# Rounding the first attention's weights on GpSimd: one instruction with two additions, or two with a multiplication and an addition each

## The chip, the cores and the metric

The kernel runs on one core of one Trainium2 chip. The metric is the device time of one execution in microseconds; the time before is the median of three runs. The profile is of one further execution, seen by the hardware profiler.

## The reference

Sixteen batch elements x[b] of 256 tokens by 256 features, each with a context of 77 tokens, pass through four blocks. Every element takes the same way, and until the recurrence no element needs another one.

```
block 0:  x = attention_q(ln1(x), itself)    + x      16 heads, quantised   ("a1")
          x = attention_q(ln2(x), context)   + x      16 heads, quantised   ("a2")
          x = geglu(ln3(x))                  + x
block 1:  x = x + attention(rms(x), itself)           ("sa")
          x = x + attention(rms(x), context)          ("ca")
          x = x + swiglu(rms(x))
block 2:  x = x + attention(ln(x), ln(tokens))        8 heads ("mh")
          u = (ln(x) @ W_in) @ B;  s_t = silu(A s_(t-1)) + u_t;  x = x + s @ C + ...
block 3:  one more attention over the context, softmax over the queries, and a layer norm
attention_q:  q, k, v rounded to 8 bits;  w = softmax(q k / 4)
              out = (round(w / d) clipped to 0..255) * d  @  v
```

The change is in `round(w / d)` of a1, the first attention. There the weights of one element are 16 heads x 256 queries x 256 keys.

## The kernel before

**Layout of the program.** It has three parts, one after the other: all sixteen elements through blocks 0 to 2 up to the recurrence's input; the recurrence; block 3. In the first part three elements are under way at a time ("streams"); each stream has buffers of its own (`work0`, `work1`, `work2`, which the profile shows as `work`).

**Who decides the order.** Each engine runs its instructions in the order in which they were written, and waits on semaphores. The order of the first part is made at build time by a small list scheduler (class `Plan`): `plan()` adds some 5,000 tasks, each with an engine, a cost in us written into the code, and the tasks it needs. `order()` starts always the task that can start earliest, and among equals the one of the oldest element and with the longest rest ahead. So a changed cost can move any task on any engine. A second plan, `plan3()`, does the same for block 3. In `plan()` a DMA transpose ("turn") occupies the queue of SyncE for `TURN` = 2.5 us, and the time in which a load or a store lands is a task of `LAND` = 2.5 us on an engine "clock" that doesn't exist on the chip.

**The first attention's chain.** a1 is done in 8 parts of an element (`(u, i)`: four units u of a half of the heads and a tile of 128 queries, two halves i each; a part is 128 queries x 4 heads x 256 keys = 128x1024). Each part goes: TensorE scores (L882) -> VectorE maximum (L1191, L1194) -> ScalarE exponentials (L1440, four instructions) -> VectorE reciprocal, factor (L1276, L1278) and four scalings to multiples of the step, clipped at 255 (L1285) -> GpSimd rounding (L775) -> SyncE's queue issues a DMA transpose (L687) -> TensorE weighs the values (L954), once for each half of the heads, when the four parts of that half have landed. The rounding adds 1.5 * 2^23 and takes it away again, which leaves the nearest whole number, and writes it as bf16:

```python
eng.tensor_scalar(rounded_part(a, u, i, p), e_part(a, u, i, p), MAGIC, -MAGIC, ALU.add, ALU.add)
```

There are two buffers for the scaled weights and two for the rounded ones (`HELD` = 2): the scores of a part stand in the plan behind the rounding two parts before it, and its rounding waits for the transpose two parts before it. Behind the weighing come ScalarE's L1462 (`xhat`), the output projection (L836), VectorE's residual (L1308), and the norm of the second attention. The second attention, a2, has 4 parts of 128x616; VectorE rounds these (L1296), and their transposes and weighing have the same lines 687 and 954, the weighing with 77 rows in place of 128.

**GpSimd's other work** in this part: the factor of each norm (L734), a bias added to the residual (L741), the spread of the rounded keys and queries (L749, L760), one scaling of a2's weights (L767), a memset (L728). In block 3, L1667 spreads the queries.

## Time and profile before

| | us |
|---|---|
| median of 3 runs (lowest, highest) | 3125.79 (3118.36, 3126.36) |
| the profiled execution's own time | 3128.91 |
| span of its trace, first to last instruction | 3127.2 |
| TensorE busy | 2520.2 |
| VectorE busy | 1899.8 |
| ScalarE busy | 1297.8 |
| GpSimd busy | 1023.1 |

PE is TensorE's matmuls and PEld its weight loads, DVE VectorE, ACT ScalarE, POOL GpSimd, SPq SyncE's queue. "Busy" is the time in which an instruction of the engine runs. The idle time before an instruction is put down to what ended it (the releaser); "issue" is time in which the engine waited for nothing that the profile shows. L775 is line 775 of the kernel.

### The profile page before, as it was taken

The numbers are of one execution on the slowest core, as the hardware profiler recorded it, in microseconds if no ns is written. First come the engines' busy times: TensorE is split into PE (matmuls) and PEld (weight loads), VectorE is DVE, ScalarE is ACT, GpSimd is POOL, SyncE is SP. The second block draws the span as 40 slices with busy tenths as digits, with TensorE's granted clock in tenths as the row PEclk, the third lists the DMA queues.
The fourth block names the chain that finished last, engine by engine and source line by source line (L and its number), as shares of the span: only waits on it lengthen the run. The fifth ranks groups of instructions, "written<-read, shape, count | busy, mean of one in ns | idle before, by whom it ended". The sixth has DMA issues, their size and how long they took to land. (4 is left out here: it accounts for less than half of the span.)

```text
span 3127.2 us, 47208 instructions
## 1 busy us (share of the span) xinstructions
PE 2520.2 (81%) x16568; PEld 1811.3 (58%) x16568; DVE 1899.8 (61%) x4639; ACT 1297.8 (42%) x3243; POOL 1023.1 (33%) x903
## 2 busy tenths in 40 slices
PE   4369888898888888898989898888888765448997
PEld 3247676666666766575767666666666442334443
DVE  4975666776766576868686767676764320004766
ACT  1534344545443345454444544344432211224654
POOL 3841132423242233343333334242321010005775
PEclk9679898898888989898989898979888765558999
DMA  4220011101111011111111111110110000001110
GB/s 187 45 52 10 20 18 24 38 21 21 31 31 24 18 28 31 31 25 27 35 24 29 30 24 28 23 28 22 28 25 7 5 18 23 0 0 34 35 37 22
DMA packets 222407, 90.45 MB, mean 29 GB/s; under 512 B 205280, under 2 KB 212784, under 8 KB 221424
## 3 DMA queue, kind: packets, MB, share of 16 engines
q1 hardware_dynamic: 215728, 67.68, 10.9%
q10 hardware_dynamic: 6464, 19.93, 1.7%
q8 instruction: 132, 2.16, 0.3%
q14 instruction: 83, 0.68, 0.1%
HBM read 27.80 MB, written 9.44 MB: 12 GB/s over the span
## 5 line engine op out<-in xcount | busy, mean ns | idle before, releaser
L775 POOL TENSOR_SCALAR work<-work 128x1024 bf16<-128x1024 f32 x128 | 466.6, 3650 | 319.4 <-DVE work L1285 260.6
L1002 PE MATMUL psum<-hT,w_l 128*128 128x256 f32 x2048 | 490.1, 397 | 19.2 <-ACT hT L1356 9.4
L1002 PEld LDWEIGHTS psum<-hT,w_l 128*128 128x128 f32 x2048 | 401.6, 199 | 90.5 <-ACT hT L1356 14.0
L734 POOL TENSOR_TENSOR rstd<-ms,half 128x2 f32<-128x2 f32 (+1 forms) x144 | 101.5, 706 | 850.1 <-DVE ms L1089 446.1
L1456 ACT ACTIVATE work<-psum 128x1024 f32<-128x1024 f32 (+1 forms) x224 | 222.0, 1021 | 284.9 <-PE psum L934 251.8
L1440 ACT ACTIVATE work<-psum,nbias,qs 128x256 f32<-128x256 f32 x512 | 281.6, 565 | 122.4 <-DVE nbias L1194 120.4
L827 PE MATMUL psum<-hT,w_l 128*128 128x256 f32 x896 | 249.4, 433 | 14.7 <-ACT hT L1356 13.5
L836 PE MATMUL psum<-w_l,xhat 128*128 128x256 f32 x640 | 198.2, 464 | 50.1 <-DVE xhat L1265 34.7
L1014 PE MATMUL psum<-w_l,work 128*128 128x256 f32 x1024 | 231.9, 385 | 2.4 <-DVE work L1318 2.1
L827 PEld LDWEIGHTS psum<-hT,w_l 128*128 128x128 f32 x896 | 189.7, 219 | 58.1 <-issue 18.7
L1356 ACT ACTIVATE hT<-psum,cols 128x256 f32<-128x256 f32 x256 | 121.9, 530 | 230.4 <-PE psum L818 229.3
L1014 PEld LDWEIGHTS psum<-w_l,work 128*128 128x128 f32 x1024 | 194.4, 192 | 37.1 <-DVE work L1318 5.2
L1191 DVE TENSOR_REDUCE nmax<-psum 128x8 f32<-128x616 f32 (+1 forms) x192 | 206.3, 1074 | 8.3 <-PE psum L882 8.3
L1308 DVE TENSOR_TENSOR x_res<-x_res,psum 128x512 f32<-128x512 f32 x112 | 76.7, 685 | 210.6 <-PE psum L1014 149.5
L1558 PE MATMUL psum<-w_l,a_pad 128*64 x508 | 99.2, 276 | 130.7 <-ACT w_l L1570 130.7
L836 PEld LDWEIGHTS psum<-w_l,xhat 128*128 128x128 f32 x640 | 143.0, 233 | 95.1 <-DVE xhat L1265 46.5
L818 PE MATMUL psum<-ident,xhat 128*128 128x128 f32 x512 | 95.5, 317 | 100.1 <-DVE xhat L1103 49.7
L1208 DVE TENSOR_REDUCE nmp<-psum 128x4 f32<-128x1024 f32 x128 | 148.3, 1215 | 39.7 <-PE psum L896 39.5
L1285 DVE TENSOR_SCALAR work<-work,rsum 128x256 f32<-128x256 f32 x512 | 164.7, 384 | 4.5
L1784 DVE TENSOR_TENSOR w_l<-w_l,psum 128x512 f32<-128x512 f32 x16 | 10.8, 674 | 256.1 <-PE psum L1723 256.1
L1558 PEld LDWEIGHTS psum<-w_l,a_pad 128*64 128x64 f32 x508 | 73.3, 206 | 158.1 <-issue 158.1
L767 POOL TENSOR_TENSOR work<-work,rsum 128x616 f32<-128x616 f32 x64 | 79.5, 1242 | 258.6 <-DVE rsum L1278 244.6
(183 smaller groups left out, 4719.7 us busy)
## 6 DMA issues: line engine op xcount, KB each, us to landing
w_l<-in_w_l ACTq DMA_DIRECT2D x1, 5120.0 KB, 25.1
x_res<-in_x SPq DMA_DIRECT2D x16, 256.0 KB, 2.8
res<-x_res ACTq DMA_DIRECT2D x16, 256.0 KB, 2.4
w_l<-res SPq DMA_DIRECT2D x16, 256.0 KB, 2.8
out<-w_l ACTq DMA_DIRECT2D x16, 256.0 KB, 2.0
w_l<-in_w_l ACTq DMA_DIRECT2D x1, 3072.0 KB, 13.4
work<-work SPq DMA_TRANSPOSE x192, 3.1
w_l<-in_w_l SPq DMA_DIRECT2D x2, 1024.0 KB, 8.5
```

Of the source, the lines that this page charges most:

```text
L775: eng.tensor_scalar(rounded_part(a, u, i, p), e_part(a, u, i, p), MAGIC, -MAGIC, ALU.add, ALU.add) \
L827: mm = eng.matmul(banks.tile(key)[:, ft * n:(ft + 1) * n], wt[:, k, ft * P:(ft + 1) * P], src(k), start=(k == 0), stop=(k == KT - 1))
L836: mm = eng.matmul(banks.tile(key)[0:n, m * D:(m + 1) * D], src(k, m), wt[:, k, :], start=(k == 0), stop=(k == KT - 1))
L1002: mm = eng.matmul(banks.tile(key)[:, h * TOKENS:(h + 1) * TOKENS], w1[:, k, h, m * P:(m + 1) * P], hT[p][:, k, :], start=(k == 0), stop=(k ...
L1014: mm = eng.matmul(banks.tile(key)[:, tt * D:(tt + 1) * D], actT(p)[:, m, tt * P:(tt + 1) * P], w2[:, m, :], start=(m == 0), stop=(m == MT ...
L1191: eng.tensor_reduce(m, s, X, ALU.max, negate=True).then_inc(*norm_step.next(("max", a.name, u, i, p)))
L1208: eng.tensor_reduce(nmp[p][:, half, tile, 64 * i:64 * i + 64:16], s.rearrange("p r (j n) -> p (r j) n", j=2), X, ALU.max, negate=True).the ...
L1285: ins = eng.tensor_scalar(e, e, rsum[:, r, h:h + 1], 255.0, ALU.mult, ALU.min)
L1356: eng.activation(dst, banks.tile(key)[:, ft * n:(ft + 1) * n], ACT.Identity, bias=col(b, ft) if b else 0.0, scale=col(g, ft)) \
L1440: ins = eng.activation(e[:, h * TOKENS:(h + 1) * TOKENS], s[:, h, :], ACT.Exp, bias=nbias[:, r, h:h + 1], scale=qs[:, ATTENTIONS.index(a), ...
L1456: eng.activation(pt(n, p)[0:a.kp, :], banks.pair(key)[0:a.kp, :, :].rearrange("p r n -> p (r n)"), ACT.Exp) \
L1558: eng.matmul(z[0:STATE, n, :], a_pad[:, 0:STATE], G[:, :, n], start=False, stop=True, skip_group_check=True).then_inc(ag_done, 1)
```

## The change

It does three things.

1. Rounding of a1 on GpSimd takes two instructions. The first multiplies by 1.0 and adds 1.5 * 2^23, in float32, in place; it signals a new semaphore `even`, and GpSimd itself waits for that. The second adds -1.5 * 2^23, multiplies by 1.0 and writes bf16. The wait for the transpose of two parts before now stands between the two, no longer ahead of both.
2. The scheduler's costs: the rounding 2.25 us in place of 2.05; a transpose occupies SyncE's queue for 1.25 us and lands 2.0 us after that (before: occupies it for 2.5 us, landing included); loads and stores have the 2.0 us as a lag of their own, no longer 2.5 us on the one "clock".
3. By that the order of the first part is a new one on every engine. The order of block 3 is the same as before.

```diff
@@ Plan
-        self.us[task], self.after[task], self.fills[task] = us, [t for t in after if t], fills
+        self.us[task], self.after[task], self.fills[task], self.lag[task] = us, [t for t in after if t], fills, lag
-            rest[t] = self.us[t] + max([HOP + rest[f] for f in followers[t]], default=0.0)
+            rest[t] = self.us[t] + self.lag[t] + max([HOP + rest[f] for f in followers[t]], default=0.0)
-                    soonest[f] = max(end[b] + HOP * (b[0] != f[0]) for b in self.after[f])
+                    soonest[f] = max(end[b] + self.lag[b] + HOP * (b[0] != f[0]) for b in self.after[f])
@@ plan(), quantised attention
-                e = work.add("pool" if a.self_attn else "vector", "round", a, (u, i), p, 2.05 if a.self_attn else 1.0, e,
+                e = work.add("pool" if a.self_attn else "vector", "round", a, (u, i), p, 2.25 if a.self_attn else 1.0, e,
                              turned.get(2 * u + i - HELD))
-                turned[2 * u + i] = work.add("sync", "turn", a, (u, i), p, TURN, e,
-                                             weighed if a.self_attn else None, v if a.self_attn else None)
+                turned[2 * u + i] = work.add("sync", "turn", a, (u, i), p, 1.25, e,
+                                             weighed if a.self_attn else None, v if a.self_attn else None, lag=LAND)
@@ plan(), loads
-        x = work.add("clock", "stored", None, 0, p, LAND, earlier(p, "scalar", "store", None, 0)) if p >= STREAMS else None
-        x = work.add("sync", "load", "x", 0, p, 0.3, x)
-        x = work.add("clock", "loaded", "x", 0, p, LAND, x)
+        x = work.add("sync", "load", "x", 0, p, 0.3, earlier(p, "scalar", "store", None, 0), lag=LAND)
@@ gpsimd, round_off
-                    if 2 * u + i >= HELD:
-                        eng.wait_ge(*turned[part_slot(u, i, p)].at((a.name, *before(u, i), p)))
                     eng.wait_ge(*norm_step.at(("up", a.name, u, i, p)))
-                    eng.tensor_scalar(rounded_part(a, u, i, p), e_part(a, u, i, p), MAGIC, -MAGIC, ALU.add, ALU.add) \
-                        .then_inc(*probs_ready_p.next((a.name, u, i, p)))
+                    e = e_part(a, u, i, p)
+                    eng.tensor_scalar(e, e, 1.0, MAGIC, ALU.mult, ALU.add).then_inc(*even.next((a.name, u, i, p)))
+                    eng.wait_ge(*even.at((a.name, u, i, p)))
+                    if 2 * u + i >= HELD:
+                        eng.wait_ge(*turned[part_slot(u, i, p)].at((a.name, *before(u, i), p)))
+                    eng.tensor_scalar(rounded_part(a, u, i, p), e, -MAGIC, 1.0, ALU.add, ALU.mult) \
+                        .then_inc(*probs_ready_p.next((a.name, u, i, p)))
```

**TensorE, the last weighing of a1 for the tenth element** (stream 0: `work0`, `vpad0`). Before, behind the scores of its last two parts (L882) stand the weighing of the first half of the heads (the first L954), eight pieces of other streams, and the weighing of the second half:

```order
L882 MATMUL psum<-work0 128x256 x8
L954 MATMUL psum<-work0,vpad0 32x256 x16
L827 MATMUL psum<-ctxT,w_l0 128x77 x4
L836 MATMUL psum<-w_l2,xhat1 128x256 x4
L818 MATMUL psum<-ident,xhat2 128x128 x4
...
L896 MATMUL psum<-work2 128x256 x28
L918 MATMUL psum<-ident,nmp2 128x128 x2
L954 MATMUL psum<-work0,vpad0 32x256 x16
```

Of the change (its lines from here on are one or two off: L883 is the scores, L955 the weighing), at the same place, the scores of the last part alone, and the weighing:

```order
L883 MATMUL psum<-work0 128x256 x4
L980 MATMUL psum<-work2,vpad2 32x256 x8
L837 MATMUL psum<-w_l1,xhat2 128x256 x4
L837 MATMUL psum<-w_l2,ctxT 77x256 x2
L819 MATMUL psum<-ident,xhat1 128x128 x4
L828 MATMUL psum<-hT1,w_l0 128x256 x8
L819 MATMUL psum<-ident,xhat2 128x128 x4
L955 MATMUL psum<-work0,vpad0 32x256 x16
```

Between the last scores and the weighing stood 78 matmuls; now 30 stand there. From the tenth element on the order of before repeats itself with every element, that of the change with every second one: at the eleventh element more stands between the two again.

**GpSimd, the roundings of the same element.** Before, its last four:

```order
L775 TENSOR_SCALAR work0<-work0 128x1024 x3
L734 TENSOR_TENSOR rstd1<-ms1,half 128x2
L775 TENSOR_SCALAR work0<-work0 128x1024
L741 TENSOR_TENSOR x_res1<-x_res1,rows 128x512
L734 TENSOR_TENSOR rstd2<-ms2,half 128x2
L734 TENSOR_TENSOR rstd1<-ms1,half 128x2
L741 TENSOR_TENSOR x_res1<-x_res1,rows 128x512
L775 TENSOR_SCALAR work0<-work0 128x1024
L760 TENSOR_SCALAR work1<-kc,par 128x154 x2
L775 TENSOR_SCALAR work0<-work0 128x1024
```

Of the change, its last three, each now two instructions (L772, L776):

```order
L758 TENSOR_SCALAR work1<-kc,par 128x154 x2
L772 TENSOR_SCALAR work0<-work0 128x1024
L776 TENSOR_SCALAR work0<-work0 128x1024
L732 TENSOR_TENSOR rstd1<-ms1,half 128x2
L732 TENSOR_TENSOR rstd5<-ms5,half 77x1
L772 TENSOR_SCALAR work0<-work0 128x1024
L776 TENSOR_SCALAR work0<-work0 128x1024
L772 TENSOR_SCALAR work0<-work0 128x1024
L776 TENSOR_SCALAR work0<-work0 128x1024
```

The last two roundings now stand directly behind each other, and two norm factors (L732, one of them of the element in stream 1) stand ahead of them.

## Rows read from the trace of the kernel before

**Rows 1.** The page: busy time, and the 40 slices.

```profile
span 3127.2 us, 47208 instructions
...
PE 2520.2 (81%) x16568; PEld 1811.3 (58%) x16568; DVE 1899.8 (61%) x4639; ACT 1297.8 (42%) x3243; POOL 1023.1 (33%) x903
...
PE   4369888898888888898989898888888765448997
```

**Rows 2.** Stretches: each engine's busy time and instructions, TensorE clock, DMA share.

```profile
0.00:200.00 200.00, 88.31 (x491) 62.02 (x492) 137.34 (x322) 70.87 (x216) 110.67 (x84) 0.76 0.36 103
200.00:1111.00 911.00, 794.20 (x5522) 601.66 (x5525) 595.83 (x1466) 397.05 (x832) 273.65 (x189) 0.88 0.12 24
1111.00:2301.00 1190.00, 1044.20 (x7298) 779.65 (x7300) 851.24 (x2052) 544.07 (x1187) 411.27 (x269) 0.88 0.14 27
```

**Rows 3.** The same view, five elements of the steady part, summed.

```profile
sum 734.00, PE 649.16 PEld 485.30 DVE 533.48 ACT 334.38 POOL 252.99; mean PE 129.83 PEld 97.06 DVE 106.70 ACT 66.88 POOL 50.60
```

**Rows 4.** TensorE's waits, 1258 to 1992 us: total, times, longest.

```profile
PE psum L818 <- DVE xhat L1103: 14.2, 5, 2.8
PE psum L836 <- DVE xhat L1265: 13.6, 5, 2.7
PE psum L954 <- DMA work<-work: 9.7, 6, 1.8
```

**Rows 5.** A timeline piece: the wait that comes back with each element.

```profile
1474.32 0.40 PE L954 MATMUL psum<-work,vpad 77*32 77x256 bf16 x8 [1.72 <-DMA work<-work]
```

**Rows 6.** Timeline pieces: waits of the first attention's weighing.

```profile
124.04 1.04 PE L954 MATMUL psum<-work,vpad 128*32 128x256 bf16 x16 [11.39 <-DMA work<-work]
...
159.42 0.83 PE L954 MATMUL psum<-work,vpad 128*32 128x256 bf16 x12 [7.50 <-DMA work<-work]
...
950.17 0.51 PE L954 MATMUL psum<-work,vpad 128*32 128x256 bf16 x12 [3.64 <-DMA work<-work]
```

**Rows 7.** Groups of instructions, whole run: GpSimd's and the first attention's.

```profile
L1002 PE MATMUL psum<-hT,w_l 128*128 128x256 f32 x2048 | 490.1, 397 | 19.2 <-ACT hT L1356 9.4 <-DVE work L1318 4.8 <-DVE x_res L1308 3.3
L775 POOL TENSOR_SCALAR work<-work 128x1024 bf16<-128x1024 f32 x128 | 466.6, 3650 | 319.4 <-DVE work L1285 260.6 <-DMA work<-work 51.4 <-DVE rden L1276 7.4
...
L1440 ACT ACTIVATE work<-psum,nbias,qs 128x256 f32<-128x256 f32 x512 | 281.6, 565 | 122.4 <-DVE nbias L1194 120.4 <-issue 1.3
...
L1285 DVE TENSOR_SCALAR work<-work,rsum 128x256 f32<-128x256 f32 x512 | 164.7, 384 | 4.5
...
L1667 POOL TENSOR_SCALAR work<-x_res,mask 128x256 f32<-128x256 f32 x256 | 118.9, 483 | 60.1 <-ACT x_res L1886 47.7 <-PE psum L1744 8.8 <-PE psum L1714 3.6
...
L1278 DVE TENSOR_SCALAR rsum<-rden,qs 128x4 f32<-128x4 f32 x128 | 56.7, 443 | 4.7
...
L760 POOL TENSOR_SCALAR work<-work,par 128x512 bf16<-128x512 f32 x32 | 22.2, 701 | 31.4 <-DVE work L1117 31.4
...
L749 POOL TENSOR_SCALAR work<-work 128x512 bf16<-128x512 f32 x32 | 19.9, 621 | 92.4 <-DVE work L1117 92.4
...
L760 POOL TENSOR_SCALAR work<-kc,par 128x154 bf16<-128x154 f32 x32 | 12.8, 409 | 47.3 <-DVE kc L1117 46.1 <-PE psum L818 0.8 <-PE psum L827 0.3
```

**Rows 8.** Line 775 alone, by stretch: busy time and count.

```profile
0.00:200.00 200.00, 72.77 (x20) 0.76 0.36 103
200.00:1111.00 911.00, 152.64 (x42) 0.88 0.12 24
1111.00:2301.00 1190.00, 241.21 (x66) 0.88 0.14 27
```

**Rows 9.** Timeline of GpSimd during the start: roundings back to back.

```profile
109.64 14.47 POOL L775 TENSOR_SCALAR work<-work 128x1024 bf16<-128x1024 f32 x4 [4.63 <-DVE rden L1276]
```

**Rows 10.** Lines 687 and 1278: duration ns min/median/max; landing of the transposes.

```profile
L687 SPq DMA_TRANSPOSE work<-work x192: 1231/1233/1935, 67.7 to 2359.3; - x192
...
DMA to landing us min/median/max: 3.0/3.1/4.8
...
L1278 DVE TENSOR_SCALAR rsum<-rden,qs x192: 228/231/1259, 62.5 to 2353.3; 128x4 f32<-128x4 f32 x128, 128x8 f32<-128x8 f32 x64
```

More of the change, by code:

```diff
@@ L26 @@
 LAG = 3.0
-TURN, LAND = 2.5, 2.5
+LAND = 2.0
 HOP = 0.15
@@ L79, in __init__, with add @@
     def __init__(self):
-        self.us, self.after, self.fills = {}, {}, {}
-    def add(self, engine, kind, what, part, p, us, *after, fills=()):
+        self.us, self.after, self.fills, self.lag = {}, {}, {}, {}
+    def add(self, engine, kind, what, part, p, us, *after, fills=(), lag=0.0):
         task = (engine, kind, what, part, p)
-        self.us[task], self.after[task], self.fills[task] = us, [t for t in after if t], fills
+        self.us[task], self.after[task], self.fills[task], self.lag[task] = us, [t for t in after if t], fills, lag
         return task
@@ L280, in context_of @@
             before = [earlier(p, "tensor", "context_" + what, MH, 0) for what in ("keys", "values")]
-            before = [work.add("clock", "loaded", "ctx", 0, p, LAND, work.add("sync", "load", "ctx", 0, p, 0.3, *before))]
+            before = [work.add("sync", "load", "ctx", 0, p, 0.3, *before, lag=LAND)]
             before.append(("scalar", "store", None, 0, p - STREAMS - 1) if p > STREAMS else None)
@@ L310, in plan @@
         used = [("tensor", "context_" + what, CA, 0, p) for what in ("keys", "values")]
-        c = work.add("sync", "load", "tok", 0, p, 0.3, earlier(p, "tensor", "norm", "lnc", 0))
-        c = work.add("clock", "loaded", "tok", 0, p, LAND, c)
+        c = work.add("sync", "load", "tok", 0, p, 0.3, earlier(p, "tensor", "norm", "lnc", 0), lag=LAND)
         c = work.add("vector", "moments", "lnc", 0, p, 0.5, c, *late)
@@ L322, in plan @@
         u = work.add("scalar", "drive", None, 0, p, 0.5, u)
-        work.add("scalar", "store", None, 0, p, 0.1, u, bias)
+        work.add("scalar", "store", None, 0, p, 0.1, u, bias, lag=LAND)
     return work
@@ L619, in build @@
         act_ready = sig("act_ready")
+        even = sig("even")
         uT_ready = sig("uT_ready")
@@ L771, in round_off @@
                     u, i = part
+                    eng.wait_ge(*norm_step.at(("up", a.name, u, i, p)))
+                    e = e_part(a, u, i, p)
+                    eng.tensor_scalar(e, e, 1.0, MAGIC, ALU.mult, ALU.add).then_inc(*even.next((a.name, u, i, p)))
+                    eng.wait_ge(*even.at((a.name, u, i, p)))
                     if 2 * u + i >= HELD:
                         eng.wait_ge(*turned[part_slot(u, i, p)].at((a.name, *before(u, i), p)))
-                    eng.wait_ge(*norm_step.at(("up", a.name, u, i, p)))
-                    eng.tensor_scalar(rounded_part(a, u, i, p), e_part(a, u, i, p), MAGIC, -MAGIC, ALU.add, ALU.add) \
+                    eng.tensor_scalar(rounded_part(a, u, i, p), e, -MAGIC, 1.0, ALU.add, ALU.mult) \
                         .then_inc(*probs_ready_p.next((a.name, u, i, p)))
```

## The prediction

> **What bounds the kernel now.** I read the page first: in a span of 3127.2 us TensorE is busy 81%, GpSimd 33%, and the slices show TensorE at eight or nine tenths from 200 us to about 2400 [rows 1]. So a faster GpSimd instruction helps only where TensorE, or an engine that feeds it, waits for it. The busy times by stretch say where to look. In the first 200 us TensorE is busy 88.3, VectorE 137.3, GpSimd 110.7; from 200 to 1111 us TensorE is at 794.2 of 911 (87%), from 1111 to 2301 at 1044.2 of 1190 (88%), with VectorE next at 72% and GpSimd at 35% [rows 2]. Line 775 runs 20, 42 and 66 times in these three, which is all of its 128 [rows 8]; the recurrence and block 3 behind them hold none and keep their order, so I cost them at nothing.
>
> Then the steady part: five elements in 734 us, 146.8 us each, of which TensorE is busy 129.8 and idle 17.0 [rows 3]. Its waits there are for the norms (14.2 us for L1103), for the tail of the other attentions (13.6 for L1265), and 9.7 us in 6 waits for a transpose's landing ahead of L954 [rows 4]. The last looks like our rounding, but is not: the wait that returns with each element stands before the weighing with 77 rows, which is a2's, and VectorE rounds that [rows 5]. Five such of 1.7 us make 8.7 of the 9.7. A1's weighing waits long only early: 11.39 and 7.50 us in the start, and three times between 3.3 and 3.7 us from 200 to 1111 us, one of which is shown [rows 6].
>
> **The change, part by part.** *The price of one rounding.* Two additions on 128x1024 take 3.650 us [rows 7], 3.56 ns for an element of a partition. The trace has no instruction that multiplies first and then adds, and none that adds and then multiplies at 1024. The nearest rows add first and multiply then: 128x512 in 0.621 us with constants (L749), 0.701 us with a factor from SBUF, and 128x154 of that kind in 0.409 (L760); two multiplications to float32 on 128x256 take 0.483 (L1667) [rows 7]. From the two L760 rows an element costs 0.82 ns, so 128x1024 takes 0.621 + 512 x 0.82 ns = 1.04 us; in proportion to L749 it would be 1.24 at most. I take 1.1 us for each of the two, and 2.2 us for the pair with the wait on `even` (its own engine's last instruction: some hundredths). That is 1.45 us less than now. The bounds: 0.9 us each below, by the slope between L1667 and L749 (0.54 ns), which is 1.85 less for the pair; above, if the form that multiplies first is as slow as two additions, 3.65 + 1.1 = 4.75, which is 1.1 us more. I take the low value, since three forms with a multiplication all lie near 1 to 2 ns for an element, and only the one with none in it is slow.
>
> The Trainium skill ("GPSIMD Engine Reference", Performance pitfalls for Q7 kernels) says that a chain of dependent fp32 operations costs 4 cycles for an element. By that any two dependent operations, an addition and a multiplication too, would take some 3.4 us at 1024 elements, an estimate from the page, and two such instructions 6.8: the change would lose 3.2 us for a part. L749, which is such a pair at 1.2 ns for an element, speaks against it here.
>
> *GpSimd's own time* falls by 128 x 1.45 = 186 us of 1023. It is idle two thirds of the time, so this is worth only what the three stretches show.
>
> *The start.* Here roundings of several streams queue up: four in a row take 14.47 us [rows 9], and 18.9 us of waits stand before two weighings [rows 6]. Each row of four saves 5.8 us if all of it is on the path; half of the waits' total is more than 9. I take 10 us; bounds 3 (the scores wait for ScalarE and VectorE all the same) and 19.
>
> *200 to 1111 us.* Three waits of 3.3 to 3.7 us, each behind one or two roundings in series: 1.45 to 2.9 us less each, 7 us in all; bounds 4 and 11.
>
> *Steady part.* What a1's rounding costs TensorE here is at most 9.7 - 8.7 = 1 us in five elements. In the order of before the work that hides it is what stands between the last scores and the weighing. I take 0 to 1 us.
>
> *VectorE.* L1278 handles 4 numbers a partition: median 0.231 us [rows 10], mean 0.443 [rows 7]. L1285 likewise has a mean of 0.384. I read this as VectorE held up while GpSimd runs. It loses 128 x 0.21 = 27 us on L1278, and GpSimd's busy time falls by 18%, its longest instruction by two thirds: perhaps 10 us of it come back, and as much on the lines like it. A quarter of that on the path: 5 us, bounds 0 and 15.
>
> *The wait for the transpose* now stands between the halves, so the first half runs during it: of 51.4 us in 10 waits [rows 7] about 1.1 us each, 11 us of GpSimd's time. In the steady part it is hidden like the rest.
>
> *The order.* Nearly every task of the first part moves. The transposes cost the scheduler 2.5 us before, on the queue; they occupy it 1.233 us and land after 3.1 [rows 10], which the new 1.25 + 2.0 is close to. The rounding was planned at 2.05 and took 3.65; 2.25 is right if my price is. Both errors made the plan of before expect a1's weights 2.2 us too early; the plan of the change has no such error. But the new order also has less between scores and weighing. I take 0 for the likeliest case and let this term make the range: one microsecond more or less for an element's period of 146.8 is 15 us. From the stretch of 200 to 1111 us, where other orders run at 87% busy too, I take plus or minus 2 us for a period, thus 30.
>
> **The sum.** 10 + 7 + 0 + 5 = 22 us less. Against the profiled execution's 3128.9 us that is 3107; its time lies 3.1 above the median of the runs, so for the median I say 3104.
>
> **Rivals.** (A, the forecast) Early waits shrink, the new order is no worse than the old: 3104, own range 3085 to 3116. Chance 0.38.
>
> (B) The new order is also better: the plan now knows the latency, and of the 17.0 us that TensorE idles in each element [rows 3] 2 to 4 go. Over some 13 periods that is 26 to 52 more: about 3065. For it speaks that the waits for L1103 and L1265 are chains of latency that a truer plan could fill; against, that nothing in the plan's costs for those lines changed. Chance 0.19.
>
> (C) Given back: the early waits end on VectorE instead (it is busier than TensorE in the start [rows 2]), or the order loses what the rounding wins: 3117 to 3135, middle 3124. Chance 0.20.
>
> (D) Slower, by the new order's thin place: 30 matmuls stand between the tenth element's last scores and its weighing, where 78 stood. Fourteen of them are like L1002, whose 490.1 us for 1024 matmuls (two records each) make 0.48 us [rows 7], thus 6.7 us; with the 16 small ones about 9. The chain beside them is a maximum (I take 1.2 us), four exponentials of 0.565, the factor 0.23, four scalings of 0.384, the rounding 2.2, the landing 3.1: 10.5 us if no engine is taken [rows 7, 10]. VectorE is busy 73% of the time [rows 3], so 3 to 5 us of queueing are likely. TensorE then waits 2 to 6 us at every second element, six times, 12 to 36 us, and the norm of a2 behind it is as late. It decides against the change once it passes the 22 us won, that is from some 4 us each time. With a period longer by 3 us in all: 3145. Chance 0.18.
>
> (E) The multiplication first is as slow as two additions: a rounding of 4.75, 1.1 us more, and in the thin place of (D) it is on the path each time: 10 us lost at the start and early instead of won, and 30 at the six places: about 3165. Against it speak L749, L760 and L1667; for it, that no row shows that very form. The skill's rule above, if it held, would end here too, and higher. Chance 0.05.
>
> **The numbers.** About 0.3% (9 us) is what a measurement of this kernel can tell from no change: the three runs alone lie 8 us apart. Faster are A (but for a tenth of it) and B: 0.55. No change: C and a rest of A and D: 0.23. Slower: most of D, and E: 0.22. From 3060 to 3150 lie A, C, nearly all of B, and more than half of D.
>
> **What would show it.** In the trace after: L772 and L776 at 1.0 to 1.2 us each (near 3.6: E). TensorE's two long waits at L955 before 200 us at half their length, and 200 us busier than 88 us of 200. L1278's mean nearer to its median. In the steady part two periods in turn; if the wait before L955 with 128 rows appears there at every second element with more than 4 us, D is at work; if TensorE's idle time per element is clearly under 17 us, B. The stretch behind 2301 us should keep its length. I would be wrong mostly by the order: it moves all engines, and its term is a guess at a spread, not a reading.

## The result: slower by 1.1%, by the order and not by the instructions

The changed kernel takes 3156.64 us (median of four runs, 3155.64 to 3159.76); the kernel before, run beside it, 3122.23 (3118.36 to 3126.36). The ratio is 1.0112, with a 95% interval of 1.0093 to 1.013. That is 53 us above the forecast, and some 7 above the upper end of the range. The profiled execution took 3156.79 us.

The page of the changed kernel, the lines that answer to [rows 1]:

```profile
span 3155.1 us, 47318 instructions
...
PE 2505.0 (79%) x16568; PEld 1809.4 (57%) x16568; DVE 1897.4 (60%) x4639; ACT 1284.1 (41%) x3234; POOL 827.0 (26%) x1031
```

GpSimd is busy 196 us less (I had said 186), and the span is 28 us longer. TensorE is busy 15 us less for the same 16568 matmul records, so it is idle 43 us more.

GpSimd's and VectorE's groups of the changed kernel, to be read against [rows 7]:

```profile
L1286 DVE TENSOR_SCALAR work<-work,rsum 128x256 f32<-128x256 f32 x512 | 160.3, 376 | 4.6
...
L776 POOL TENSOR_SCALAR work<-work 128x1024 bf16<-128x1024 f32 x128 | 135.1, 1055 | 10.6
L772 POOL TENSOR_SCALAR work<-work 128x1024 f32<-128x1024 f32 x128 | 134.2, 1049 | 399.2 <-DVE work L1286 387.5 <-DVE rden L1277 11.7
...
L1279 DVE TENSOR_SCALAR rsum<-rden,qs 128x4 f32<-128x4 f32 x128 | 57.3, 448 | 4.5
```

Each new instruction takes 1.05 us. The mean of L1279, which I had expected to fall with GpSimd's load, stays at 448 ns (443 before), and the scalings stay at 376 (384).

Where the 28 us are is best read from the stores of each element's residual, which end an element. Line 1491 of the changed kernel, and the same line (1490) of before; "first to last" is the start in us of the first and the last of the 16:

```profile
L1491 ACTq DMA_DIRECT2D res<-x_res x16: 587/597/598, 370.8 to 2599.1; - x16
```

```profile
L1490 ACTq DMA_DIRECT2D res<-x_res x16: 592/597/720, 371.0 to 2571.1; - x16
```

The first stores come at the same time, the last ones 28.1 us apart; behind the last store both take 556 us more, as forecast. In between, the stores that end the steady elements, in the changed kernel's timeline:

```profile
1244.52 0.60 ACTq L1491 DMA_DIRECT2D res<-x_res  x1
...
1405.80 0.60 ACTq L1491 DMA_DIRECT2D res<-x_res  x1
...
1551.70 0.60 ACTq L1491 DMA_DIRECT2D res<-x_res  x1
...
1713.15 0.60 ACTq L1491 DMA_DIRECT2D res<-x_res  x1
...
1863.85 0.60 ACTq L1491 DMA_DIRECT2D res<-x_res  x1
...
2026.93 0.60 ACTq L1491 DMA_DIRECT2D res<-x_res  x1
```

The periods are 161.3, 145.9, 161.5, 150.7 and 163.1 us: two in turn, as forecast, and 156.5 in the mean where before had 146.8 [rows 3]. The start, and the same five periods whole, by stretches (columns as in [rows 2]):

```profile
0.00:200.00 200.00, 82.86 (x499) 59.26 (x500) 147.21 (x342) 73.08 (x224) 85.10 (x109) 0.74 0.37 106
...
1244.50:2027.00 782.50, 670.73 (x4709) 508.18 (x4709) 526.13 (x1272) 331.91 (x717) 186.84 (x207) 0.88 0.12 25
```

And the kernel before from its seventh store to its twelfth, for the count of matmuls:

```profile
1258.80:1993.30 734.50, 649.66 (x4592) 485.75 (x4591) 533.98 (x1282) 334.85 (x730) 253.49 (x171) 0.89 0.14 28
```

These five periods are 48 us longer. TensorE has 117 matmul records more in them (parts of other elements, done at other times now) and is busy 21 us more; idle it is 111.8 us, 22.4 for an element, where it was 84.8, 17.0. The stretches around give 20 us back: the changed kernel reaches the first of these stores at 1244.5 us, before at 1258.8, and gains another 6 behind them. In the start TensorE is busy 82.9 us of 200, less than before (88.3), where I had said more.

What TensorE waits for from 1405 to 2027 us (four elements; [rows 4] have five):

```profile
PE psum L837 <- DVE xhat L1266: 16.2, 5, 4.8
PE psum L819 <- DVE xhat L1102: 14.0, 6, 4.7
PE psum L828 <- ACT hT L1357: 9.1, 8, 2.0
PE psum L955 <- DMA work<-work: 7.0, 2, 3.5
PE psum L955 <- issue: 6.4, 2, 3.2
```

For one element L837 now waits 4.1 us (L836 2.7 before), and a new wait for ScalarE's `hT` costs 2.3. L819 waits 3.5 for norms, all of them those of line 1102; before it was as long, 2.8 for those of L1103 [rows 4] and 0.9 for those of L1101, which is line 1102 of the changed kernel:

```profile
PE psum L818 <- DVE xhat L1101: 4.4, 5, 1.2
```

So which norm TensorE waits for has changed, and not for how long. L955's seven and 6.4 us are, as before, ahead of a2's weighing with 77 rows, and not of a1's. Three of these four waits:

```profile
1503.24 0.40 PE L955 MATMUL psum<-work,vpad 77*32 77x256 bf16 x8 [3.54 <-DMA work<-work]
...
1596.27 0.40 PE L955 MATMUL psum<-work,vpad 77*32 77x256 bf16 x8 [3.19 <-issue]
...
1812.12 0.62 PE L955 MATMUL psum<-work,vpad 77*32 77x256 bf16 x8 [3.50 <-DMA work<-work]
```

They were 1.7 us in each element [rows 5], and are 3.2 to 3.5 here (twice put down to "issue", though it is the same wait). No wait of the weighing with 128 rows for a transpose is left in the steady part.

### The profile page after: what moved, and what is told of

Read it like the earlier page. It is cut to its first block and busy times, and to the rows that moved or that the text cites. A ratio compares the mean times of both kernels' runs of the same rounds, so it can differ in the third digit from the quotient of the medians.

```text
span 3155.1 us, 47318 instructions
## 1 busy us (share of the span) xinstructions
PE 2505.0 (79%) x16568; PEld 1809.4 (57%) x16568; DVE 1897.4 (60%) x4639; ACT 1284.1 (41%) x3234; POOL 827.0 (26%) x1031
## 3 DMA queue, kind: packets, MB, share of 16 engines
q1 hardware_dynamic: 215728, 67.68, 10.7%
## 5 line engine op out<-in xcount | busy, mean ns | idle before, releaser
L1003 PE MATMUL psum<-hT,w_l 128*128 128x256 f32 x2048 | 497.6, 404 | 17.5 <-ACT hT L1357 13.7
L1003 PEld LDWEIGHTS psum<-hT,w_l 128*128 128x128 f32 x2048 | 412.6, 204 | 93.3 <-issue 20.4
L732 POOL TENSOR_TENSOR rstd<-ms,half 128x2 f32<-128x2 f32 (+1 forms) x144 | 100.7, 700 | 1019.1 <-DVE ms L1090 651.3
L828 PE MATMUL psum<-hT,w_l 128*128 128x256 f32 x896 | 261.3, 448 | 29.9 <-ACT hT L1357 28.9
L837 PE MATMUL psum<-w_l,xhat 128*128 128x256 f32 x640 | 201.2, 470 | 53.7 <-DVE xhat L1266 46.1
L828 PEld LDWEIGHTS psum<-hT,w_l 128*128 128x128 f32 x896 | 194.6, 225 | 79.8 <-issue 31.5
L772 POOL TENSOR_SCALAR work<-work 128x1024 f32<-128x1024 f32 x128 | 134.2, 1049 | 399.2 <-DVE work L1286 387.5
L1192 DVE TENSOR_REDUCE nmax<-psum 128x4 f32<-128x1024 f32 (+1 forms) x192 | 205.9, 1072 | 13.6 <-PE psum L883 13.5
L837 PEld LDWEIGHTS psum<-w_l,xhat 128*128 128x128 f32 x640 | 147.4, 239 | 101.0 <-DVE xhat L1266 58.1
L819 PE MATMUL psum<-ident,xhat 128*128 128x128 f32 x512 | 96.0, 319 | 98.0 <-DVE xhat L1102 61.7
L1900 ACT ACTIVATE work<-psum,nmax 77x256 f32<-77x256 f32 x256 | 117.9, 464 | 89.0 <-DVE nmax L1791 87.7
```

What stands on the lines that cost most here:

```text
L772: eng.tensor_scalar(e, e, 1.0, MAGIC, ALU.mult, ALU.add).then_inc(*even.next((a.name, u, i, p)))
L828: mm = eng.matmul(banks.tile(key)[:, ft * n:(ft + 1) * n], wt[:, k, ft * P:(ft + 1) * P], src(k), start=(k == 0), stop=(k == KT - 1))
L837: mm = eng.matmul(banks.tile(key)[0:n, m * D:(m + 1) * D], src(k, m), wt[:, k, :], start=(k == 0), stop=(k == KT - 1))
L1003: mm = eng.matmul(banks.tile(key)[:, h * TOKENS:(h + 1) * TOKENS], w1[:, k, h, m * P:(m + 1) * P], hT[p][:, k, :], start=(k == 0), stop=(k ...
L1192: eng.tensor_reduce(m, s, X, ALU.max, negate=True).then_inc(*norm_step.next(("max", a.name, u, i, p)))
L1900: eng.activation(pt3(b)[0:CTX, ft * 8 + 2 * g + h, :], s_[:, h, :], ACT.Exp, bias=nmax[0:CTX, r, h:h + 1], accum_out=sums[0:CTX, r, h:h + ...
```

## The experiments

Times are medians; each kernel ran beside the kernel before on the same chip, and the ratio is to that. Where two kernels ran on different chips, the ratios compare them better than the medians. "Old" and "new" stand for the order of before and of the change.

| kernel | order, costs | rounding | us | ratio [interval] |
|---|---|---|---|---|
| the change | new | 2 instructions | 3156.6 | 1.0112 [1.0093, 1.013] |
| e1_instructions | old | 2 | 3094.4 | 0.9907 [0.9884, 0.9929] |
| e2_order | new | 1 | 3168.4 | 1.0141 [1.0118, 1.0165] |
| e3_round_cost | old, rounding 2.25 | 2 | 3109.0 | 0.9964 [0.9951, 0.9976] |
| e4_turn_cost | old, transposes 1.25 + 2.0 | 2 | 3131.0 | 1.0022 [1.0007, 1.0037] |
| e5_load_lag | old, loads and stores lag 2.0 | 2 | 3155.8 | 1.0113 [1.0086, 1.0141] |
| e8_lag25 | old, loads and stores lag 2.5 | 2 | 3091.5 | 0.9912 [0.9895, 0.9928] |
| e6_full_lag25 | new, all lags 2.5 but the transposes' | 2 | 3137.7 | 1.0051 [1.0031, 1.007] |
| e12_lag30 | new, these lags 3.0 | 2 | 3148.2 | 1.0061 [1.004, 1.0082] |
| e9_three | old | 3 | 3134.5 | 1.0048 [1.0031, 1.0065] |
| e7_slow_first | old | 2, the first with two additions | 3213.9 | one run |
| e10_four_new_order | new, fourth buffer for x | 2 | 3147.4 | 1.0068 [1.0051, 1.0085] |
| e11_four_old_order | old, fourth buffer for x | 2 | 3095.3 | 0.9895 [0.9868, 0.9923] |
| e13_less_vector_new | new, VectorE's scalings cut | 2 | 3124.8 | 1.0014 [0.9997, 1.0032] |
| e14_less_vector_old | old, same cut | 2 | 3074.0 | 0.9844 [0.9818, 0.987] |

### Which half: e1_instructions and e2_order

e1 is the kernel before with the new instructions and its own plan; e2 is the changed kernel with the old instruction.

```diff
 e1, on the kernel before:
-                    eng.tensor_scalar(rounded_part(a, u, i, p), e_part(a, u, i, p), MAGIC, -MAGIC, ALU.add, ALU.add)
+                    eng.tensor_scalar(e, e, 1.0, MAGIC, ALU.mult, ALU.add).then_inc(*even.next((a.name, u, i, p)))
+                    eng.wait_ge(*even.at((a.name, u, i, p)))
...
+                    eng.tensor_scalar(rounded_part(a, u, i, p), e, -MAGIC, 1.0, ALU.add, ALU.mult)
 e2, on the changed kernel: the same backwards
```

> The two rounding instructions alone: the scheduler's costs and so the order of every engine are those of before. Theory 1 (the order is what made the change slower, the instructions are a small gain): the ratio to before lies at 0.993 to 0.998, thus 3100 to 3116 us, the two long waits ahead of L954 in the first 200 us shrink by a third or more, and the period of the steady part stays at 146.5 to 147 us. Theory 2 (the second instruction and its wait on the semaphore cost more than they save, by VectorE that is held up or by GpSimd's queue): above 3126, up to the 3157 of the change.

> The other half: all costs and thus the order of the change, but the rounding in one instruction with two additions, as before. Theory 1: slower than the change itself, 3165 to 3190 us, since the new order keeps its long periods (146 and 162 us in turn) and the rounding is 1.5 us longer in it. Theory 2: near before, 3115 to 3135.

The instructions alone win 29 us (e1 lies 6 us below the range that I had given it); the order alone loses 44, and under the new order the instructions win only 12. So the loss is the order's: 62 us between e1 and the change, which have the same instructions. By their pages TensorE is idle 650.1 us in the change and 586.5 in e1, and busy 2505.0 and 2508.8: the whole loss is idle time of TensorE.

Where e1 wins, by its stores (line 1494), against the row of L1490 above:

```profile
L1494 ACTq DMA_DIRECT2D res<-x_res x16: 597/597/603, 363.9 to 2539.0; - x16
```

By the first store it is 7.1 us ahead, by the last 32.1. Its timeline puts the seventh store at 1240.9 us (17.9 ahead) and the twelfth at 1974.7 (18.6), so the steady part gives nothing, and 13.5 come in the last four elements: 10.2 of them in the two periods up to the fourteenth store, which still hold 17 of the 128 roundings and three elements under way, and 3.3 behind the last rounding. Its windows, the start and the five steady periods:

```profile
0.00:200.00 200.00, 91.05 (x512) 64.42 (x513) 141.36 (x331) 74.92 (x226) 82.34 (x106) 0.77 0.38 106
...
1240.90:1974.70 733.80, 655.59 (x4592) 489.39 (x4591) 525.86 (x1281) 335.12 (x730) 191.59 (x210) 0.89 0.14 28
```

The first 200 us have TensorE busy 91.1, 3 more than before. The four waits of its weighing for a transpose there fall from 22.1 to 16.0 us in all, while those of the scores for ScalarE's exponentials rise from 21.2 to 28.4: on these two lines nothing is won.

The windows show something that the stores hide. In the five steady periods TensorE is idle 78.2 us in e1 and 84.8 before, but busy 655.6 and 649.7 for the same 4592 matmul records, at a granted clock of 0.886 of full speed in place of 0.893 (the view rounds both to 0.89). e3, e8, e11 and e14, whose steady part has nearly or exactly this order and the same two instructions, have 78 us idle and 656 to 657 busy there too. In the last four elements it goes the other way: TensorE is busy 480.5 us before and 472.1 in e1 for the same matmuls, at a mean clock of 0.81 and 0.84. Of the 31.9 us between the two traces 20.5 are idle time of TensorE and 11.4 are matmuls that took less. Each is one trace, and no run holds the clock still, so why the steady period keeps its length isn't shown.

### What the rounding costs where: e9_three and e7_slow_first

Both have the order of before. e9 puts a third short instruction in front; e7 gives the first one the two additions, so that it takes as long as before's, and the second comes on top.

```diff
 e9, on e1:
+                    eng.tensor_scalar(e, e, 1.0, 0.0, ALU.mult, ALU.add).then_inc(*even.next((a.name, u, i, p, "extra")))
+                    eng.wait_ge(*even.at((a.name, u, i, p, "extra")))
                     eng.tensor_scalar(e, e, 1.0, MAGIC, ALU.mult, ALU.add)
 e7, on e1:
-                    eng.tensor_scalar(e, e, 1.0, MAGIC, ALU.mult, ALU.add)
+                    eng.tensor_scalar(e, e, 0.0, MAGIC, ALU.add, ALU.add)
```

> The order of before and the two new instructions, with a third ahead of them that multiplies by 1.0 and adds 0.0 in place: the value is the same, GpSimd's rounding takes three times 1.05 us and its two semaphore waits, some 3.3 us, as against 2.1 in the run of the instructions alone and 3.65 before. Theory 1 (the length of the rounding is what counts): the gain of 29 us mostly goes, 3112 to 3122 us. Theory 2 (the slow form with two additions itself harms VectorE beside it, whatever it takes): the gain stays, 3090 to 3103, and VectorE's L1278 has the mean of the run of the instructions alone.

> The order of before, the first of the two instructions with two additions (0.0 and 1.5 * 2^23) in place of multiplication and addition, float32 to float32; the second as in the change. If the form with two additions is slow whatever it writes and whatever its constants are, it takes 3.6 to 3.7 us and a rounding 4.7, the run 3135 to 3150. If what was slow before was the conversion to bf16 behind two additions, it takes 1.1 us, and the run is at 3090 to 3100. Under the view that a slow instruction holds VectorE up only in its first and last microsecond, VectorE's instructions that start in its middle keep their usual length.

e9 is 40 us slower than e1 (44 by the ratios), above both ranges that I had given, though its steady periods stay at 147 us, and 14 slower than the kernel before beside it, whose one instruction is longer than e9's three together. What got longer in its groups is VectorE's rows:

```profile
L1291 DVE TENSOR_SCALAR work<-work,rsum 128x256 f32<-128x256 f32 x512 | 170.4, 395 | 4.5
...
L775 POOL TENSOR_SCALAR work<-work 128x1024 f32<-128x1024 f32 x128 | 135.3, 1057 | 353.6 <-DVE work L1291 338.8 <-DVE rden L1282 14.8
L777 POOL TENSOR_SCALAR work<-work 128x1024 f32<-128x1024 f32 x128 | 134.4, 1050 | 10.6
L781 POOL TENSOR_SCALAR work<-work 128x1024 bf16<-128x1024 f32 x128 | 133.8, 1045 | 10.6
...
L1284 DVE TENSOR_SCALAR rsum<-rden,qs 128x4 f32<-128x4 f32 x128 | 63.6, 497 | 4.5
```

L1284 (which is L1278 of before) has gone from 415 ns in e1 to 497, and the scalings from 364 to 395. A rounding here is the three rows' 3.15 us, and before 3.65 gave 443 and 384; VectorE is busy 1933.6 us in all, before 1899.8. So it isn't how long GpSimd works; how much of that holds VectorE is the reading that fits, and the last section shows the holding itself. The trace is of the fastest of e9's four runs (3125.9; the others 3134 to 3136), and it puts the loss at the start: the first store is 8 us behind before's, the twelfth 7, the last 3 ahead.

e7's groups and its longest wait from 200 to 2400 us:

```profile
L775 POOL TENSOR_SCALAR work<-work 128x1024 f32<-128x1024 f32 x128 | 469.0, 3664 | 284.3 <-DVE work L1289 273.6 <-DVE rden L1280 10.8
```

```profile
PE psum L958 <- DMA work<-work: 49.9, 22, 4.8
```

Two additions take 3.66 us with float32 output and a constant of 0.0 too. Now a rounding takes 4.7 us and the steady periods are 153 to 158 us, with TensorE waiting for transposes 22 times; with 2.1, 3.15 and 3.65 us they are the same 147. In the steady part a1's weighing now waits 1.5 to 2.9 us for a transpose at every element, where it had one wait of 1 us in five before, so what hides the rounding there in the old order ends between 3.65 and 4.7 us. But these waits are 11 of the 46 us that the five periods have grown by:

```profile
1295.90:2076.40 780.50, 679.12 (x4592) 502.20 (x4591) 553.27 (x1280) 334.60 (x730) 294.90 (x210) 0.85 0.13 26
```

TensorE is idle 16.5 us more than before and busy 29.5 us more, at a granted clock of 0.85 in place of 0.89. VectorE is held longer too (L1282 566 ns in the mean, the scalings 443). It is a single run, 64 us above the range that I had given, and I have no account of that time beyond these rows.

### Which cost makes the order: e3, e4, e5, e8

Each takes e1 and gives the scheduler one of the change's costs. e8 writes the loads and stores as e5 does, but leaves their landing at 2.5 us.

```diff
 e3:
-                e = work.add("pool" if a.self_attn else "vector", "round", a, (u, i), p, 2.05 if a.self_attn else 1.0, e,
+                e = work.add("pool" if a.self_attn else "vector", "round", a, (u, i), p, 2.25 if a.self_attn else 1.0, e,
 e4:
-                turned[2 * u + i] = work.add("sync", "turn", a, (u, i), p, TURN, e, ...)
+                turned[2 * u + i] = work.add("sync", "turn", a, (u, i), p, 1.25, e, ..., lag=2.0)
 e5, and e8 with lag=2.5 (likewise the context's load, the tokens' and the store):
-        x = work.add("sync", "load", "x", 0, p, 0.3, x)
-        x = work.add("clock", "loaded", "x", 0, p, LAND, x)
+        x = work.add("sync", "load", "x", 0, p, 0.3, earlier(p, "scalar", "store", None, 0), lag=2.0)
```

> The two new instructions with the costs of before, but for the rounding at 2.25 in place of 2.05 us. TensorE's order is nearly that of before and repeats with every element in the steady part. Theory 1 (what harms is the pattern that repeats with every second element): within 10 us of the instructions alone, 3085 to 3105. Theory 3 (any change of the order costs, since the costs of before had been tuned to a lucky order): 3110 to 3150.

> The new instructions with the costs of before, but for the transposes: 1.25 us of SyncE's queue and a lag of 2.0. The loads' and stores' 2.5 us and the rounding's 2.05 stay. The order has no steady pattern any more within the last elements. Theory 1a (the loads' shorter lag made the bad order): 3095 to 3125 us. Theory 1b (the transposes' cost did): 3140 to 3165.

> The new instructions with the costs of before, but for loads and stores: a lag of 2.0 us in place of 2.5 us on the one clock. Transposes stay at 2.5 us of the queue, the rounding at 2.05. TensorE's order is close to the change's and repeats with every second element. Theory 1a (the loads' shorter lag made the bad order): 3140 to 3165 us, periods of about 147 and 161 us in turn, and a chain of store, load and first norm ahead of the long waits. Theory 1b: 3100 to 3125.

> The two new instructions, all costs of before, but loads and stores with a lag of their own of 2.5 us in place of the task of 2.5 us on the one clock. TensorE's order is that of before but for few tasks and repeats with every element. Theory 1a (it is the shorter lag, 2.0, and not the way of writing it, that made the order with two elements): 3085 to 3105 us. Otherwise 3140 to 3165.

Half a microsecond on the landing of loads and stores, of which an element has a handful, is enough for the whole loss: e5 is as slow as the change (3155.8), e8 as fast as e1. In e5 TensorE's waits from 1405 to 2027 us are the change's to the tenth of a microsecond, two of the five rows shown above:

```profile
PE psum L837 <- DVE xhat L1266: 16.2, 5, 4.8
...
PE psum L955 <- DMA work<-work: 7.0, 2, 3.5
```

The notation did nothing (e8). The rounding's cost alone loses 15 us (18 by the ratios), the transposes' alone 37; e3 and e4 lie between the ranges of their two theories and decide neither. These losses don't add up: each cost gives another order. That of e5 is the change's in the steady part (841 of TensorE's 1680 tasks in one row, from the seventh element to the fifteenth), that of e8 is before's in all but the first element or so (1594 in one row); e1, e7, e9, e11 and e14 have before's order on every engine, e2, e10 and e13 the change's.

### Would a truer plan be better: e6, e12

From the fourth element on the x load lands 2.5 to 4.3 us after its issue in the changed kernel, the store 2.3 or more, so 2.0 is too short. Both kernels keep the change's rounding and transposes and lengthen that lag.

```diff
-LAND = 2.0
+LAND = 2.5        (e6; e12: 3.0; the transposes keep 2.0)
```

> The change with one number put back: loads and stores lag 2.5 us in place of 2.0; transposes 1.25 + 2.0, rounding 2.25 stay. The order has no pattern that repeats with one or two elements. Theory 1a (the loads' 2.0 alone makes the harm): 3095 to 3130. Theory 3 (any order but that of before costs about as much): 3140 to 3165.

> The change with a lag of 3.0 us for loads and stores in place of 2.0, closer to what they take in the trace (2.3 for the store, 2.5 to 4 for the load); transposes 1.25 + 2.0 and rounding 2.25 stay. The order differs much from both others. Theory 1b (too short a lag is the harm): below 3110. Theory 3 (the costs of before happen to give a good pattern, and most other orders are 20 to 60 us worse, whatever their truth): 3120 to 3165.

They win 19 and 8 us back (e12 16 by the ratios; e6 lies between the ranges of its theories), and stay 43 and 54 behind e1. A plan nearer to the measured durations is not a faster one here: of eight sets of costs run with the new instructions, the two with before's (e1, e8) are the fastest, and the other six lie 15 to 62 us above e1.

There is a number that does tell them apart, and I overlooked it: the end of the plan itself, which `order()` keeps as `self.length`. Worked out from `plan()` of each kernel, in us:

| | e8 | e1 | e3 | e4 | e12 | e6 | e5 | the change |
|---|---|---|---|---|---|---|---|---|
| end of the plan | 2466.2 | 2471.6 | 2486.5 | 2501.7 | 2509.7 | 2511.7 | 2524.2 | 2529.6 |
| measured | 3091.5 | 3094.4 | 3109.0 | 3131.0 | 3148.2 | 3137.7 | 3155.8 | 3156.6 |

e1's plan is that of the kernel before. The plan of the change ends 58 us later by its own costs, and it measured 62 later; e3's ends 15 later and measured 15; that of e5, whose one changed cost is a shorter one, ends 53 later and measured 61. Only e6 and e12, 2 us apart in the plan and 10 on the chip, change places. So the scheduler made a worse plan from shorter landings, and its own number told so. I read this behind the runs, from eight plans of one kernel; it was not tried as a forecast.

### What in the new order costs: e10 to e14

Two suspects stood out. In the changed kernel the next element's load follows each store at once and is waited for; the queue's waits from 200 to 2400 us, before and after:

```profile
SPq L670 <- DMA res<-x_res: 53.6, 4, 24.6
```

```profile
SPq L668 <- DMA res<-x_res: 229.4, 13, 27.2
```

e10 and e11 break that chain with a fourth buffer for x, under either order, so that a load waits for the store of four elements before.

```diff
-        x_res = [sb(f"x_res{p}", [P, TT, D]) for p in range(STREAMS)] * BATCH
+        x_res = [sb(f"x_res{p}", [P, TT, D]) for p in range(STREAMS + 1)] * BATCH
...
-                        if b >= STREAMS:
-                            eng.wait_ge(*r_stored[b % STREAMS].at(b - STREAMS))
+                        if b > STREAMS:
+                            eng.wait_ge(*r_stored[(b - STREAMS - 1) % STREAMS].at(b - STREAMS - 1))
```

> The change with a fourth buffer for x, so that the load of an element no longer waits for the store of the one three before it, but for the one four before; to make room, a constant that nobody reads shares a buffer and two small sums share one. Order and costs are those of the change. Theory 1b (the plan puts store, load and first norm in a row with 4.3 us, the chip takes 6.1 to 7, and all engines stand behind it): the long periods of 161 us shrink by 5 us or more, 3115 to 3140 us. Theory 4 (the load is not it; the new order has less work of one element beside that of another at many places): 3145 to 3158.

> The control: the same fourth buffer on the new instructions with the order of before. Both theories: within 5 us of the instructions alone, 3087 to 3100, since there the load lands ahead of what needs it.

Under the new order it wins 9 us by the medians, 14 by the ratios; under the old one nothing (1 us more by the medians, 4 less by the ratios). So this chain costs about 10 of the 62. But it costs them ahead of the steady part: e10's seventh store is 12.7 us ahead of the change's and its last one 12.9, and its five steady periods are the same 161, 146, 161, 151 and 163 us, with the same waits of TensorE. The long periods, which I had expected to shrink by 5 us or more if this chain made them, did not.

The other suspect is VectorE: the new order puts stretches in which it is the busy one beside others in which it has nothing to do. Two of the changed kernel's:

```profile
1457.00:1470.00 13.00, 6.00 (x53) 3.73 (x52) 11.91 (x28) 4.76 (x12) 3.50 (x6) 0.74 0.13 26
1636.00:1662.00 26.00, 26.00 (x124) 22.93 (x123) 7.61 (x19) 9.18 (x18) 0.70 (x1) 1.00 0.06 11
```

From 1457 to 1470 us VectorE is busy 92% and TensorE 46%, and from 1636 to 1662 the two MLPs stand back to back, with TensorE at 100% and VectorE at 29%. In the order of before the third attention of the element ahead lies between them. The idle time sits in the short periods more than in the long: from 1405.8 to 1551.7 us TensorE is idle 28.1 us, in the 161 us behind it 20.4. e13 and e14 take VectorE's work off, by scaling one head of four in each part of a1.

```diff
-                    for h in range(4):
+                    for h in range(1):
                         e = e_part(a, u, i, p)[:, h * TOKENS
```

> The change with three of VectorE's four scalings of a part's weights left out (so three heads of four are rounded unscaled): VectorE has 384 instructions of 0.36 us less, some 8.7 us for each element. Theory 5 (the new order loses its 62 us in stretches where VectorE works for several attentions at once and TensorE starves, while its long MLP stretches leave VectorE idle): it gains clearly more than the order of before does by the same cut, 80 us or more, and the two come to lie within 35 us of each other. Theory 6 (the loss is latency at many places, whoever works there): both gain about as much, and the distance stays 50 to 70 us.

> The control: the same three scalings left out of the two new instructions with the order of before. Theory 5: a gain of 30 to 60 us on 3094. Theory 6: the same gain as in the new order, so that the distance between the two stays 50 to 70 us.

They leave three of four heads unscaled, so their results are not those of the reference. The cut wins 32 us under the new order, 20 under the old, and the distance between the orders shrinks from 62 to 51. VectorE's load carries about 11 of it, no more: the 80 us that theory 5 asked for under the new order did not come.

## Why the prediction was wrong

**The order was the step that failed.** I wrote "I take 0 for the likeliest case and let this term make the range", and "plus or minus 2 us for a period, thus 30". It measured 62 us on top of the new instructions, 44 with the old one. I had read the size from other stretches at 87% busy; the steady periods grew by 9.7 us where I allowed 2, and of the 9.7 us 5.4 are idle time of TensorE. The size could be read in the two plans, which end at 2471.6 and 2529.6 us, and I did not look there. I had also argued that "the plan of the change has no such error" in the weights' latency, and let that stand against the thin place. It weighed nothing: with 2.1 to 3.65 us for a rounding the steady periods of the old order are the same, so a plan that knows it exactly wins nothing there, while the shorter landing of loads and stores, which I mentioned in the change and never priced, brings the slow order by itself (e5, e8).

**The price of a rounding was right.** 1.05 us for each where I took 1.1, and the form that multiplies first is no slower (E is out).

**Start, 200 to 1111 us and the end.** For the instructions alone, the sum was 22 us and e1 wins 29. The start gave 7 and not 10; 10.7 came from there to 1259 us (7.6 of them up to the sixth store at 1111.6, where I said 7); nothing in the steady part, as I said, but not as I said it: 6.6 us of idle time went there and came back as busy time. Missed were 13.5 us in the last four elements: I took the steady part's cover for all of 1111 to 2301 us. Of these, 8.4 are TensorE busy less for the same matmuls. Of the 32 us that e1's whole trace is shorter, 11 are such busy time. My sum has no term for it, so that the 22 came near e1's 29 is in part luck. In the change itself none of the start's gain is left: TensorE waits there for its weighing 26.0 us and for ScalarE's exponentials 30.6 (before 22.1 and 21.2):

```profile
PE psum L883 <- ACT work L1441: 30.6, 9, 9.5
...
PE psum L955 <- DMA work<-work: 26.0, 4, 8.6
```

**VectorE: 5 us, wrong.** L1279 kept its mean. Two short instructions hold VectorE about as long as the slow one (below). Under the old order there is a little relief, 415 ns in e1:

```profile
L1289 DVE TENSOR_SCALAR work<-work,rsum 128x256 f32<-128x256 f32 x512 | 154.5, 364 | 4.6
...
L1282 DVE TENSOR_SCALAR rsum<-rden,qs 128x4 f32<-128x4 f32 x128 | 53.2, 415 | 4.5
```

That is 3.6 us on L1282 and 10 on the scalings, so I can't exclude a share of it in e1's 29; under the changed order only 4 us on the scalings are left.

**Rival D had the sign, and the wrong place.** Its mark, a wait ahead of L955 with 128 rows at every second element, doesn't occur. What comes back in its place is a2's wait (3.2 to 3.5 us), and longer waits for `hT` and for the tail of the attentions. The thin place that I priced is wide enough even for the slow rounding: e2, with 3.65 us in the same order, has one such wait of 1.3 us in its five steady periods. That D's 3145 came within 12 us of the result is luck, and E's 3165 lay nearer still, by a cause that is out.

**What stays open.** Of the 62 us, about 10 are the chain of store, load and first norm, about 11 are VectorE's load, if the two can be added. The other 40 lie in many waits, none over 5 us in the steady part. I showed that the landing cost alone brings this order there, not which of its moves costs the rest; no experiment moved a single task. Periods of 160 us and more beside others of 146 come back in e4, e6 and e12 too.

## What to carry to other kernels

Where a scheduler writes the order, an edit of its costs is a change of its own, to be priced and timed apart from the instruction that it comes with: here the instruction won 29 us and the costs beside it lost 62. Nearness of the costs to the measured durations is no evidence that the order gets better; compare the two plans' own ends before anything else (here they were 58 us apart), and time the instruction under the old order first and keep it if no new order beats it (e1 or e8, 3094.4 and 3091.5 us, 0.9% under the kernel before). And a faster instruction on an engine with cover is worth what it wins outside the steady part: here all of e1's gain came ahead of the seventh store and behind the twelfth. Where two traces have the same matmuls in the same order, compare TensorE's busy time and granted clock too, before a gain is put down to a wait.

## What the runs showed of the hardware

**Two additions are the slow pair on GpSimd, a multiplication with an addition isn't.** On 128x1024 float32, multiply-add to float32 and add-multiply to bf16 take 1.05 us each, and add-add 3.65 to bf16 and 3.66 to float32, the latter with a constant of 0.0. The Trainium skill's 4 cycles for an element of a dependent fp32 chain ("GPSIMD Engine Reference", Performance pitfalls for Q7 kernels), 3.4 us as I estimated from it, is near what two additions take and more than three times the pairs with a multiplication.

**A slow GpSimd instruction leaves VectorE alone in its middle.** The kernel before, one rounding on GpSimd, and some of VectorE's instructions under it:

```profile
1400.65 3.74 POOL L775 TENSOR_SCALAR work<-work 128x1024 bf16<-128x1024 f32 x1 [1.37 <-DVE work L1285]
```

```profile
1400.81 0.97 DVE L1117 TENSOR_SCALAR kc<-kc 128x154 f32<-128x154 f32 x1
...
1402.21 0.29 DVE L1117 TENSOR_SCALAR vc<-vc 77x256 f32<-77x256 f32 x1
...
1402.62 0.23 DVE L1278 TENSOR_SCALAR rsum<-rden,qs 128x4 f32<-128x4 f32 x1
...
1402.88 0.35 DVE L1285 TENSOR_SCALAR work<-work,rsum 128x256 f32<-128x256 f32 x1
...
1403.42 1.12 DVE L1285 TENSOR_SCALAR work<-work,rsum 128x256 f32<-128x256 f32 x1
```

The L1117 that starts 0.16 us into the rounding takes 0.97 us (0.24 where GpSimd does nothing); the three behind it, in the middle, take 0.29, 0.23 and 0.35 us; the scaling that starts 2.77 us in takes 1.12 and ends 0.15 us behind the rounding. It is so in the whole trace: 93 scalings start 0.9 to 2.5 us into a rounding and take 0.34 to 0.35 us, the 3 that start in its first 0.3 us take 1.09 to 1.11, the 11 that start more than 2.7 us in take 1.03 to 1.12 (of the 15 between 2.5 and 2.7 us some are held, some not). The same place of the same order in e9, with three short instructions:

```profile
1409.08 1.05 POOL L775 TENSOR_SCALAR work<-work 128x1024 f32<-128x1024 f32 x1 [1.29 <-DVE work L1291]
1410.20 1.05 POOL L777 TENSOR_SCALAR work<-work 128x1024 f32<-128x1024 f32 x1
1411.33 1.04 POOL L781 TENSOR_SCALAR work<-work 128x1024 bf16<-128x1024 f32 x1
```

```profile
1409.31 0.91 DVE L1123 TENSOR_SCALAR kc<-kc 128x154 f32<-128x154 f32 x1
...
1410.63 0.76 DVE L1123 TENSOR_SCALAR vc<-vc 77x256 f32<-77x256 f32 x1
...
1411.51 0.89 DVE L1284 TENSOR_SCALAR rsum<-rden,qs 128x4 f32<-128x4 f32 x1
```

Here each GpSimd instruction holds one of VectorE until 0.03 to 0.14 us after its own end: 0.91, 0.76 where before had 0.29, and 0.89 where it had 0.23. So 3.65 us of the slow form hold VectorE for about the first and the last 1.1, and two short ones for their 2.1: about the same, which fits that VectorE is busy 1897.4 us in the change and 1899.8 before. The Trainium skill ("SBUF — State Buffer", Who interferes with whom) says, of VectorE in the modes in which it uses two ports, that whoever issues first gets the pair of ports that VectorE and GpSimd share "for the whole instruction". The short instructions agree with that; the slow one doesn't, since VectorE instructions that are held at its two ends ran at full speed in its middle.
